# Four convolution layers and a residual composed into one nine-tap kernel per sample

## What is computed

```python
def _layer(x, style, w, b, mw, mb, typ):
    s = style @ mw.T + mb
    weight = SCALE * w * s[:, None, :, None]
    demod = lax.rsqrt(jnp.sum(weight * weight, axis=(2, 3)) + EPS)
    weight = weight * demod[:, :, None, None]
    if typ == 'same':
        out = jax.vmap(_conv_same)(x, weight) + b[None, :, None]
    elif typ == 'upsample':
        out = jax.vmap(_conv_up)(x, weight.transpose(0, 2, 1, 3)) + b[None, :, None]
        out = _blur(out, 2.0 * blur_k, (1, 1))
    elif typ == 'downsample':
        xb = _blur(x, blur_k, (2, 2))
        out = jax.vmap(_conv_down)(xb, weight) + b[None, :, None]
    return out
...
for i, typ in enumerate(('same', 'upsample', 'same', 'downsample')):
    out = _layer(out, style, weights[i], biases[i], mod_w[i], mod_b[i], typ)
return x + out
```

## Time and profile before

| | before |
|---|---|
| median of 3 runs, us | 757.64 (757.38 to 760.92) |
| span of the profiled execution, us | 756.7 |
| DVE busy, us | 705.7 |
| PE busy, us | 669.0 |
| POOL busy, us | 450.7 |
| ACT busy, us | 442.4 |
| mean granted PE clock | 0.965 |

### The profile page before, as it was taken

One profiled execution on the slowest core, in us unless ns is written; L12 is line 12 of the kernel. 1 busy time (PEld: TensorE's weight loads), 2 busy tenths in 40 slices (PEclk: granted clock), 3 DMA queues, 4 the chain that ended last, 5 costly groups with the idle time before them and its releaser, 6 DMA issues.

```text
span 756.7 us, 11174 instructions
## 1 busy us (share of the span) xinstructions
PE 669.0 (88%) x3348; PEld 561.5 (74%) x3348; DVE 705.7 (93%) x989; ACT 442.4 (58%) x807; POOL 450.7 (60%) x457
## 2 busy tenths in 40 slices
PE   1757799989997999999996999999998799999996
PEld 1546678878785787878775887878787687887875
DVE  6988899999999999999999999999999999999984
ACT  2455366757544676575654657666655466575763
POOL 6555356858554585767565376765755467595530
PEclk9969899999999999999999899999999899999999
DMA  7001273837545395675746347574835548393952
GB/s 264 0 0 30 56 182 113 180 112 183 137 113 120 89 190 132 145 174 115 154 132 133 113 112 176 138 160 120 161 97 141 124 132 166 111 178 112 187 133 85
DMA packets 147147, 98.39 MB, mean 130 GB/s; under 512 B 113232, under 2 KB 113616, under 8 KB 147088
## 3 DMA queue, kind: packets, MB, share of 16 engines
q1 hardware_dynamic: 146432, 96.04, 53.3%
q10 hardware_dynamic: 656, 1.64, 0.6%
HBM read 36.51 MB, written 33.62 MB: 93 GB/s over the span
## 4 chain that ended last, share of the span: by engine, by line
DVE 51%; PE 21%; issue 21%; ACT 2%; DVEq 1%; ACTq 0%
DVE xl L635 11%; DVE zl L652 10%; DVE xl L632 9%; DVE GT L667 4%; DVE T L682 4%; PE po L164 4%; PE po L166 4%; PE po L165 4%; DVE Q2f L662 3%; DVE T L681 2%; DVE HH L729 1%; PE pc L164 1%; DVE zf L645 1%; PE pc L165 1%; PE pc L166 1%
## 5 line engine op out<-in xcount | busy, mean ns | idle before, releaser
L164 PE MATMUL po<-zh,Wh 128*128 128x512 f32 x512 | 208.9, 408 | 27.1 <-DVE zl L652 18.9
L165 PE MATMUL po<-zl,Wh 128*128 128x512 f32 x512 | 206.4, 403 | 0.0
L166 PE MATMUL po<-zh,Wl 128*128 128x512 f32 x512 | 206.1, 403 | 0.0
L540 POOL TENSOR_TENSOR D<-X 128x256 f32<-128x256 f32 x128 | 92.7, 724 | 129.3 <-DVE xl L635 109.3
L411 ACT ACTIVATE T<-po,cv,DD 128x512 f32<-128x512 f32 x128 | 99.6, 778 | 91.3 <-PE po L166 91.0
L582 POOL TENSOR_TENSOR Wl<-GT,Wh 128x512 fp32r<-128x512 f32 x64 | 90.0, 1416 | 87.5 <-ACT Wh L431 87.5
L164 PEld LDWEIGHTS po<-zh,Wh 128*128 128x128 f32 x512 | 99.6, 195 | 47.9 <-issue 29.9
L635 DVE SCALAR_TENSOR_TENSOR xl<-D,S,xh 128x512 fp32r<-128x512 f32 x128 | 134.8, 1053 | 0.0
L166 PEld LDWEIGHTS po<-zh,Wl 128*128 128x128 f32 x512 | 99.7, 195 | 24.2
L165 PEld LDWEIGHTS po<-zl,Wh 128*128 128x128 f32 x512 | 99.2, 194 | 18.2
L398 ACT ACTIVATE M<-ps,b0z 128x256 f32<-128x256 f32 x128 | 60.6, 473 | 83.2 <-PE ps L166 83.2
(11 more groups left out here) (170 smaller groups left out, 1226.5 us busy)
## 6 DMA issues: line engine op xcount, KB each, us to landing
X<-in_xin SPq DMA_DIRECT2D x64, 513.0 KB, 5.2
out<-T SPq DMA_DIRECT2D x63, 513.0 KB, 4.3
Wh<-Wh SPq DMA_DIRECT2D x105, 128.0 KB, 3.7
Wl<-Wl SPq DMA_DIRECT2D x105, 128.0 KB, 3.9
E<-in_ed ACTq DMA_DIRECT2D x1, 768.0 KB, 8.6
out<-T SPq DMA_DIRECT2D x2, 256.5 KB, 4.1
GT<-in_b SPq DMA_DIRECT2D x1, 448.0 KB, 5.3
XE<-in_xe SPq DMA_DIRECT2D x1, 448.0 KB, 9.6
```

The source lines that it names most:

```text
L164: eng.matmul(o, wh_, rh, start=first, stop=False)
L165: eng.matmul(o, wh_, rl, start=False, stop=False)
L166: return eng.matmul(o, wl_, rh, start=False, stop=last)
L540: pool.tensor_tensor(D[:, b % 2, 0, :], x[:, 0:511:2], x[:, 1:512:2], ALU.subtract)
```

## The change

The four layers and the residual become one kernel of nine taps per sample. With even and odd positions on two halves of the partitions this is five blocks of weights, so `conv(b)` is 15 matmuls of 512 columns directly from `xh` and `xl`. `conv_z`, `zf`, `zh`, `zl`, `D`, `M1` and the final addition of `X` are gone; the residual is a diagonal (`ID`) added to a weight block. The split of `x` is made for two samples at once, without a scale, over 516 columns each.

Composing the weights has a third stage. Groups are of 4 samples, work is in seven units of 256-column matmuls: units 0 and 1 (layers 3 and 2), 2 and 3 (layer 1), 4 to 6 (layer 0). `SLOTS` puts them ahead of the convs: ahead of the first conv of group g stand unit 4 of group g+1 and units 0 and 1 of group g+2, ahead of the second units 5 and 6 of g+1, ahead of the third and fourth units 2 and 3 of g+2. On DVE the eviction is `full`, on ACT the high part is `high`, on POOL the low part is `low`, and `w_low` on DVE makes `Wl`. `finish` now only writes border values into `T`; it is on POOL, two pairs behind. The exchange has two halves per group, of eight DMAs in all, on SP between loads and stores. The input ring `X` has four places instead of five, and a load waits for `x_low` instead of `finish`. The border computation covers four positions per side instead of one or two. SP loads a 64-wide identity matrix (`EYE`) once.

```diff
-NG = 8
+NG = 4
 NGR = B // NG
+NC = NG * C
...
+SLOTS = [[(1, 4), (2, 0), (2, 1)], [(1, 5), (1, 6)], [(2, 2)], [(2, 3)]]
...
-                    sp.wait_ge(s_fin, n - XR + 1)
+                    sp.wait_ge(s_xl, n - XR + 1)
...
+            def cross(g, part):
+                sp.wait_ge(s_wh, 2 * g + part + 1)
+                sp.wait_ge(s_wl, 2 * g + part + 1)
+                a, e = (0, 2) if part == 0 else (2, 5)
+                f = min(e, 4)
...
+                    sp.dma_start(w[hi, a * NG:e * NG, 1, :], w[lo, a * NG:e * NG, 0, :]).then_inc(s_w[g % 2], 16)
+                    sp.dma_start(w[lo, (a + 1) * NG:(f + 1) * NG, 1, :], w[hi, a * NG:f * NG, 0, :]
+                                 ).then_inc(s_w[g % 2], 16)
...
-            for n in range(NQ):
-                g, i = divmod(n, NG // Q)
-                for v in range(4):
-                    if g + 1 < NGR and i == ((1, 1, 2, 2) if g else (0, 0, 2, 2))[v]:
-                        cross(g + 1, v)
+            for g in range(NGR):
+                n = NG // Q * g
+                if n:
+                    store(n - 1)
+                if n + 3 + XR - 3 < NQ:
+                    load(n + XR)
+                if g + 1 < NGR:
+                    cross(g + 1, 0)
                 store(n)
-                if n + XR < NQ:
-                    load(n + XR)
+                if n + 1 + XR < NQ:
+                    load(n + 1 + XR)
+                if g + 1 < NGR:
+                    cross(g + 1, 1)
...
+                    pe.wait_ge(s_wh, 2 * g + 2)
+                    pe.wait_ge(s_wl, 2 * g + 2)
+                    pe.wait_ge(s_w[g % 2], 8 * 16 * (g // 2 + 1))
+                if q == 0:
+                    pe.wait_ge(s_xh, n + 1)
+                    pe.wait_ge(s_xl, n + 1)
...
-                for j in range(4):
+                for j in range(5):
                     w = [t[:, g % 2, j * NG + i].rearrange("p r o -> p (r o)") for t in (Wh, Wl)]
-                    m = split_mm(pe, po[b % 2][:, :], w[0], w[1], zh[:, b % 2, j:j + 512], zl[:, b % 2, j:j + 512],
-                                 j == 0, j == 3)
+                    m = split_mm(pe, po[b % 2][:, :], w[0], w[1], xh[:, n % XH, q, j:j + L2], xl[:, n % XH, q, j:j + L2],
+                                 j == 0, j == 4)
                 m.then_inc(s_o, 1)
 
...
-                g, i = divmod(b, NG)
-                if b + 2 < B:
-                    conv_z(b + 2)
-                if b:
-                    conv_o(b)
-                if g + 1 < NGR:
-                    for k in range(7):
-                        if PIECE_SLOT[k] == i:
-                            piece(g + 1, k)
-                if (g, i) in groups_edge:
-                    edge(*groups_edge[(g, i)])
-
+                for x in units_of(b):
+                    unit(*x)
+                conv(b)
+                if divmod(b, NG) in edge_at:
+                    edge(*edge_at[divmod(b, NG)])
...
+            def x_high(n):
+                act.wait_ge(s_x[n % XR], 16 * (n // XR + 1))
+                if n >= XH:
+                    act.wait_ge(s_o, Q * (n - XH + 1))
+                act.copy(xh[:, n % XH], X[:, n % XR]).then_inc(s_xh, 1)
...
+                else:
+                    t_out(b - 1)
+                if b % Q == 0 and b // Q + 2 < NQ:
+                    x_high(b // Q + 2)
+                for x in units_of(b):
+                    if x[1] != 5:
+                        high(*x)
+                if i == 3 and g + 3 < NGR:
+                    q3_high(g + 3)
...
+            def finish(n):
+                pool.wait_ge(s_t, Q * (n + 1))
+                pool.wait_ge(s_ed, 5 * (n * Q // EC) + 5)
+                e = T[:, n % TR, :, :]
+                pool.tensor_copy(e[:, :, 0:2], EP[:, n * Q:(n + 1) * Q, 0:2])
+                pool.tensor_copy(e[:, :, L2 - 2:L2], EP[:, n * Q:(n + 1) * Q, 2:4]).then_inc(s_fin, 1)
...
+                if i == 0 and g + 1 < NGR:
+                    identity(g + 1)
+                for x in units_of(b):
+                    if x[1] < 4:
+                        low(*x)
+                if i == 2 and g + 3 < NGR:
+                    q3_full(g + 3)
+                if i == 3 and g + 3 < NGR:
+                    q3_low(g + 3)
+                if b % Q == 1 and b > 2 * Q:
+                    finish(b // Q - 2)
...
+            def x_low(n):
+                dve.wait_ge(s_xh, n + 1)
+                tt(xl[:, n % XH], X[:, n % XR], r32(xh[:, n % XH]), ALU.subtract).then_inc(s_xl, 1)
...
+                if b % Q == 0 and b // Q + 2 < NQ:
+                    x_low(b // Q + 2)
+                for x in units_of(b):
+                    full(*x)
+                if i == 0 and g + 1 < NGR:
+                    w_low(g + 1, 0)
+                if i == 1 and g + 1 < NGR:
+                    w_low(g + 1, 1)
```

More of the change, by code:

```diff
@@ L147, in build @@
+        s_id = sem("id")
         s_e, s_ed = sem("e"), sem("ed")
[L148 to L156 removed]
+        s_a2 = sem("a2l")
+        s_pp, s_ch, s_one, s_ms, s_sq, s_sc, s_k0, s_b1 = (
+            sem(n) for n in ("pp", "ch", "one", "ms", "sq", "sc", "k0", "b1"))
@@ L590, in _ @@
+            q3_low(0)
+            low(0, 0)
+            low(0, 1)
             q3_full(1)
             q3_low(1)
-            differences(3)
-            differences(4)
-            pool.wait_ge(s_sc, SC_CV)
-            for j in range(TR):
-                pool.memset(T[0:64, j, :, 0:1], 0.0)
+            low(0, 2)
+            low(0, 3)
+            pool.wait_ge(s_sc, SC_D)
+            pool.wait_ge(s_in["eye"], 16)
+            identity(0)
+            low(1, 0)
+            low(1, 1)
+            q3_full(2)
@@ L612, in _ @@
+            finish(NQ - 2)
+            finish(NQ - 1)
         @block.vector
@@ L742, in edge @@
+                    link(tt(v, pe_[:, 0:4 * EC].rearrange("p (b n) -> p b n", n=4), bc(DD[:, 3, cs], 4), ALU.mult))
+                    for h, n, x in ((lo, 0, 1), (hi, 2, 4)):
+                        for r, d in ((0, lo), (1, hi)):
+                            m = dve.scalar_tensor_tensor(
+                                out=EP[d, cs, n:n + 2], in0=v[h, :, r:r + 3:2], scalar=BB[h, 0, 3:4],
+                                in1=XE[h, cs, x + r:x + r + 3:2], op0=ALU.add, op1=ALU.add)
                     m.then_inc(s_ed, 1)
@@ L805, in _ @@
-            link(dve.tensor_scalar(tmp[:, 0:2], tmp[:, 0:2], -0.5, 1.5, ALU.mult, ALU.add))
-            link(tt(DD[:, 0:2], tmp[:, 0:2], RR[:, 0:2], ALU.mult))
+            full(0, 0)
+            full(0, 1)
+            dve.wait_ge(s_k0, K_B1D)
+            for h in range(2):
+                for r in range(2):
+                    a, p = 2 + 2 * h + r, slice(64 * r, 64 * r + 64)
+                    tt(B1dl[p, 0:2, h, :], b1s[p, a:a + 5:4, :], r32(B1dh[p, 0:2, h, :]), ALU.subtract)
+                    m = tt(B1dl[p, 2, h, :], b1s[p, 10 + r, :], r32(B1dh[p, 2, h, :]), ALU.subtract)
@@ L824, in _ @@
+            x_low(0)
+            full(0, 4)
+            w_low(0, 0)
+            full(0, 5)
+            full(0, 6)
+            w_low(0, 1)
+            dve.wait_ge(s_in["ed"], 16)
+            w1 = lambda t: E[0:64, 1, t, 0:64].unsqueeze(1).to_broadcast([64, 2, C])
+            link(tt(WSM1[:], w1(0), w1(1), ALU.add))
+            tt(WSM1[:], WSM1[:], w1(2), ALU.add)
             link(tt(WSM, WT[:, 2:4, 0], WT[:, 2:4, 1], ALU.add))
             tt(WSM, WSM, WT[:, 2:4, 2], ALU.add)
-            reached(dve.tensor_scalar(tmp[:, 0, :], S[:, 2, :], bias(1), 2.0, ALU.mult, ALU.mult))
@@ new lines, in _ @@
+            full(1, 2)
+            full(1, 3)
+            dve.tensor_scalar(tmp[:, 1], S[:, 2], bias(1), 2.0, ALU.mult, ALU.mult)
+            dve.wait_ge(s_pp, 4)
+            link(tt(kt[:], pe_[:, 0:128], D21[:], ALU.mult))
+            reached(tt(tmp[:, 1], tmp[:, 1], kt[:], ALU.add))
+            x_low(1)
+            link(tt(b0z[:], AA[:, 0], DD[:, 0], ALU.mult))
+            tt(D10[:], DD[:, 0], DD[:, 1], ALU.mult)
+            dve.tensor_scalar(b0z[:], b0z[:], bias(0), None, ALU.mult)
```

846 lines of the change are left out of this document (343 added, 503 removed).

## The result

The changed kernel takes **1430.14 us** (1428.52 to 1433.11, 4 runs), beside 759.28 (757.38 to 761.55) for the kernel before in the same comparison: 1.885 times as long, 95% interval 1.879 to 1.890. The span of its profiled execution is 1426.5 us. The forecast was 1431.

What follows compares the result with a forecast made beforehand. The prediction took a closed ring of waits, once a group, as the bound, with no engine's work setting the time; 62 + 38.4 + 1254.4 + 34 + 19.9 + 21.7 = 1430.4 of span gave 1431 us, range 1290 to 1550.

Steps and rivals of the forecast that it cites:

- The ring: Once a group, weight exchange waits for store, `finish` and POOL's low parts; PE idles 22.2 of 44.8 us; chance 0.84.
- both links: Exchange behind `store(2g)` and `finish(2g)`; `load(2g+4)` behind `store(2g-1)`, holding up `x_high` and `x_low`, 6.4 us a period.
- The faster rival: Second exchange half issued before POOL finishes the opening units, PE never waits: 712 us, deciding at 1.6 a group; chance 0.06.
- first conv: Start of group 0's first conv: 50.5 before, plus the third stage's work and exchange, at 62 us, 55 to 72.
- to the second group: From first conv to the second group's: load 4 issued early, `x_high` at 21.8 instead of 28.2, so 38.4 us.
- 28 periods: Groups 2 to 29 each open a full period of 44.8 us after the one before: 1254.4 us.
- group 30: Opening of group 30: no units 0 and 1 beyond group 31, so both exchange halves go back to back: 34 us.
- group 31: Opening of group 31: `finish(60)` waits for nothing late; the last exchange lands at 19.9 us.
- end: After the last group opens: 16.1 for four convs, 0.6 + 0.78 + 0.34, and 3.9 for the store: 21.7 us.
- The load's wait: ACT's `x_high` waits for the late load in each period, 6.4 us; rival that it doesn't bind: 1252 us, chance 0.05.
- The clock's 2.1: PE restarts at 1.2 GHz after each group's long idle and loses 2.1 us a period.
- the crowded value: Exchange landing 5.7 us after issue behind a store and a load, chosen over 3.0 alone, which was kept as a bound.

Runs made afterwards that it cites:

- Undone alone: From the changed kernel, SP's list reordered: both exchange halves ahead of the stores, 937.04 us; or, in another run, each load ahead of its store, 1201.13 us.
- undone together: From the changed kernel, SP's list reordered to loads, then both exchange halves, then stores: 759.43 us, ratio 1.0034 to the kernel before.
- undone together from POOL's side: From the changed kernel, POOL's list alone reordered, `finish` of both pairs ahead of the low parts: 781.04 us, ratio 1.030 to the kernel before.
- the other edits of the start: Against the 759 us order: bias computed among group 0's last units, reciprocal cut in two, low part of `B1` behind `q3_low(0)`: 750.6 us.
- filling 28 of the idles: Changed kernel plus 91 matmuls outside the result ahead of the first convs of groups 2 to 29: 1387.94 us, ratio 1.831 to the kernel before.
- the first try at filling: Changed kernel plus 75 matmuls outside the result ahead of each group's first conv from group 1 on: 1435.42 us, ratio 1.892 to the kernel before.
- the one with the load behind: Changed kernel with the load in a group's second half moved behind the weight exchange on SP: 1349.31 us, ratio 1.779 to the kernel before.

## Where the prediction was right and where not

**The ring.** Right in both links and in its place in the code. Undone alone, they give 937 and 1201; undone together, 759; and undone together from POOL's side, 781. The faster rival (712) had asked for the exchange to get out in time, which it doesn't.

**The terms of the sum.** That the total is right to 0.1% is luck in part. The terms that were too short (15.4 us) and those that were too long (19.3) cancelled, but for 3.9 us of the span; and most of that went because the median of the runs lies 3.6 us above the profiled span, where the forecast added 0.9.

| term | forecast | measured |
|---|---|---|
| first conv | 62 | 70.8 |
| to the second group | 38.4 | 43.6 |
| 28 periods | 28 x 44.8 = 1254.4 | 28 x 44.26 = 1239.4 |
| group 30 | 34 | 35.5 |
| group 31 | 19.9 | 18.8 |
| end | 21.7 | 18.6 |
| span | 1430.4 | 1426.5 |

- *First conv: mis-sized by 8.8.* The step took the first conv of before and added the work of the third stage. It left out where the new prologue puts the bias of the composed kernel: on PE its three steps stand behind the last unit of group 0 and ahead of the first conv. The weights of group 0 didn't hold up the conv; the last part of their exchange was issued at 53.54 and landed 4.3 later, at 57.8, 13 us before it. PE's wait ahead of the first of the three steps in the changed kernel is 5.7 us long, ahead of the second 1.5, ahead of the last 5.0:

```profile
PE pe L364 <- DVE tmp L753: 5.7, 1, 5.7
PE pe L371 <- DVE tmp L767: 5.0, 1, 5.0
```

  With that chain out of the way, and the other edits of the start, the first conv stood at 61.9, now behind a wait of 5.6 for POOL. The edits were made together, so how much each brings is open.

- *Second group: mis-sized by 5.2.* The step counted convs and units but not the border computation, which for the first 32 samples falls into this very group. ACT's last `T` of the group starts 25.1 us after the conv (at 95.86, the conv at 70.78) where I had 21.0. Then DVE's border steps (3.12 us of `EP`) hold up `x_low`, which starts at 99.59 though its cast ended at 97.58. 4.1 + 2.0 is 6.1, less the 0.8 by which the exchange was faster: 5.3.

```profile
95.64 3.12 DVE L678 SCALAR_TENSOR_TENSOR EP<-Y,BB,XE 64x64 f32<-64x64 f32 x4
95.86 0.77 ACT L398 ACTIVATE T<-po,cv,DD 128x512 f32<-128x512 f32 x1
...
99.59 1.22 DVE L596 TENSOR_TENSOR xl<-X,xh 128x1032 fp32r<-128x1032 f32 x1
```

- *The period: 0.5 too long.* On average over the 28 periods the second store is issued at 35.0, as forecast, and the whole 0.5 is the exchange behind it, set at 9.8 from the earlier trace rows and measured at 9.3. But the 35.0 is itself a sum of two errors: the first store came at 22.5 instead of 22.0, and the cast 5.7 behind it instead of 6.2. The load's wait, 6.4, was worth 5.4 to 5.7 once it was separated from what the load does to the exchange. The clock's 2.1 was 2.3.
- *The end: 3.1 too long.* The last `po` matmul starts 13.8 us after the group's first (1407.95 to 1421.76), which 60 matmuls at 0.234 give (59 x 0.234 = 13.8); the forecast's 16.1 still had the slow start in it. But only 1.2 us of idle come before that group, and PE began it at full pace.

**The two places where a page was weighed against a row.** After each of the long idles matmuls ran at the 1.2 GHz level, a granted clock of 0.5, for 2.7 to 6.1 us, and filling 28 of the idles gave back 42 us of 1430, or 3.0%. The Trainium skill (TensorE: Matmul & The Clock Gate, "What's actually happening") puts the ramp's penalty under 1% of a typical kernel span and says not to fit it to a specific count of slow matmuls. This kernel is not typical in that there are 30 restarts, and the measurement decides.

As for the exchange, its larger pieces landed in 5.6 to 5.7 behind a load and in 3.7 to 4.2 without, and alone before the change in 3.0. The Trainium skill (DMA: Bandwidth & Descriptors, "Why small descriptors are slow (HBM only)") says that transfers within SBUF don't suffer from small descriptors. No run here changed the size of a descriptor, so that sentence stands untested. Nor does it say that transfers land as if alone, as the prediction took it; what made these later was the load ahead of them, and to take the crowded value was right.

**The faster rival, priced too low.** Had the ring not been there, I had 712; the order without it took 759. The start and the second group are 9 us each of that. The rest is PE's own work: three more border computations at some 4 us each (groups of 23.5 and 21.7 us among those of 21.1), and 0.6 in every group, 21.1 where 116 matmuls at the paces of the earlier trace rows make 20.5. Of that 0.6, 0.2 is pace: 256-column matmuls started 0.119 apart (12 from 693.46 to 694.89 in the first try at filling the idle), not 0.115; the rest I have not traced. The point from which the change loses was therefore not 1.6 us of wait a group but about zero, and even a change that did all that was intended would not have been faster without the better start.

## What to carry to other kernels

When work moves between engines, follow each queue once round: which instruction waits for which, and whether the last one is behind the first in some queue. This ring of stores, loads and exchanges cost its full latency in every turn, while no engine was busy for more than 54%, and it could be opened in either of two queues, SP's or POOL's. Then price the start, the end and the seldom steps as carefully as the loop: here they were off by nearly 20 us without regard to sign, the long term by 15.

## What the hardware showed that I had not expected

- PE's clock fell after short idles too, and the length of the idle alone didn't tell how. In the first try at filling, after 3.80 us without a matmul the conv ran at 0.43 per 512 columns at once; after 3.11 us it ran five matmuls at 0.23 to 0.3 and then eight at 0.43, from 418.32 to 421.73; after 2.23 it kept its pace. But it kept it after 3.09 as well, fell after five matmuls behind an idle of 2.56, and was slow at once behind one of 3.33. The slow stretch behind an idle of some 20 us was not always the same either, 5.3 us from 688.07 in the changed kernel and 3.1 from 654.62 in the one with the load behind.
- One load right ahead of an exchange cost the exchange 1.5 to 1.9 us of landing, with its own issue 2.3 us a period or 63 us in all. The 16 DMA engines are busy for a third of the span, but for 88% of the time from the store to the conv: the mean hides that the transfers come in bursts, and the bursts lie on the ring.
- Useless matmuls made the kernel faster, by 3%: 1387.94 us with 583 us of them, 1430.14 without.
